# The half chunk of the second layer's hidden blocks moves from its end to its start, and the residual's rows are formed on TensorE

## The reference, cut to what matters

```python
# _L1_cond_ref: x is x1, per sequence b an expert e = lora_indices[b], rank 16, SCALE 0.5
gate = x @ W_gate.T + SCALE * (x @ A_gate[e].T) @ B_gate[e].T      # 512 -> 1376
up   = x @ W_up.T   + SCALE * (x @ A_up[e].T)   @ B_up[e].T
act  = silu(gate) * up
down = act @ W_down.T + SCALE * (act @ A_down[e].T) @ B_down[e].T  # 1376 -> 512
# _L1_ffn_ref on down:
xn = down * rsqrt(mean(down * down) + EPS)
xq = round-and-clip of xn to 8 bits by its row's largest value
wq = ternary W
y  = xq @ wq.T + b
return x1 + (down + gelu(y))
```

## Time and profile before

| | before |
|---|---|
| median of 3 runs | 1140.66 us (1136.92 to 1141.06) |
| the profiled execution | 1140.98 us |
| its span, first to last instruction | 1139.1 us |
| mean granted PE clock | 0.981 |
| PE busy | 1065.4 us (94%) |
| DVE / ACT / POOL busy | 556.1 / 307.1 / 134.4 us |

### The profile page before, as it was taken

One profiled execution on the slowest core, in us unless ns is written; L12 is line 12 of the kernel. 1 busy time (PEld: TensorE's weight loads), 2 busy tenths in 40 slices (PEclk: granted clock), 3 DMA queues, 4 the chain that ended last, 5 costly groups with the idle time before them and its releaser, 6 DMA issues.

```text
span 1139.1 us, 13740 instructions
## 1 busy us (share of the span) xinstructions
PE 1065.4 (94%) x5448; PEld 896.1 (79%) x5448; DVE 556.1 (49%) x680; ACT 307.1 (27%) x489; POOL 134.4 (12%) x178
## 2 busy tenths in 40 slices
PE   1899999999999999999889999999999999988775
PEld 0788888888888888888778888888888888877652
DVE  8855454444343444434753343343343344357876
ACT  1522121212112121212432131131131131134665
POOL 4400000000000000000140010010010010024325
PEclk9899999999999999999999999999999999998887
DMA  3776010100101010010411031030030130032103
GB/s 104 238 249 234 2 56 1 55 0 0 55 0 55 0 55 0 21 71 1 148 61 42 28 100 38 28 108 31 28 110 28 28 110 28 28 110 76 45 1 148
DMA packets 25425, 71.81 MB, mean 63 GB/s; under 512 B 5235, under 2 KB 5427, under 8 KB 25267
## 3 DMA queue, kind: packets, MB, share of 16 engines
q1 hardware_dynamic: 19762, 46.24, 11.5%
q0 software_dynamic: 5632, 25.17, 7.2%
HBM read 67.06 MB, written 4.34 MB: 63 GB/s over the span
## 4 chain that ended last, share of the span: by engine, by line
PE 86%; DVE 8%; ACT 2%; issue 2%; DMA 1%; POOL 0%; DVEq 0%; ACTq 0%; POOLq 0%
PE ps_gu L137 18%; PE ps_gu L138 18%; PE ps_gu L139 18%; PE ps_d L137 8%; PE ps_d L138 8%; PE ps_d L139 8%; PE ps_t L139 1%; PE ps_t L138 1%; PE ps_t L137 1%; PE ps_gu L837 1%; DVE h_lo L1626 1%; PE ps_t L728 1%; DVE ar_lo L1443 1%; ACT a_hi L1001 1%; ACT z_new L1091 1%
## 5 line engine op out<-in xcount | busy, mean ns | idle before, releaser
L137 PE MATMUL ps_gu<-a_hi,gu_hi 128*128 128x512 f32 x800 | 316.3, 395 | 2.2 <-DVE a_lo L1312 2.2
L138 PE MATMUL ps_gu<-a_lo,gu_hi 128*128 128x512 f32 x800 | 313.7, 392 | 0.0
L139 PE MATMUL ps_gu<-a_hi,gu_lo 128*128 128x512 f32 x800 | 312.7, 391 | 0.0
L139 PEld LDWEIGHTS ps_gu<-a_hi,gu_lo 128*128 128x128 f32 x800 | 151.1, 189 | 32.4
L137 PEld LDWEIGHTS ps_gu<-a_hi,gu_hi 128*128 128x128 f32 x800 | 151.6, 190 | 31.6 <-DVE a_lo L1312 2.3
L138 PEld LDWEIGHTS ps_gu<-a_lo,gu_hi 128*128 128x128 f32 x800 | 151.7, 190 | 28.4
L1480 DVE TENSOR_TENSOR s_act<-s_act,ps_gu 128x512 f32<-128x512 f32 x44 | 30.2, 687 | 193.7 <-PE ps_gu L139 193.5
L1347 DVE TENSOR_TENSOR s_act<-s_act,ps_gu 128x512 f32<-128x512 f32 x56 | 38.4, 686 | 148.0 <-PE ps_gu L139 148.0
L311 POOL DMA_INDIRECT lr_raw<-in_tab_l,rows x48 | 45.8, 955 | 369.1 <-PE ps_t L728 346.3
L137 PE MATMUL ps_d<-h_hi,dn_hi 128*128 128x512 f32 x224 | 87.6, 391 | 0.0
L139 PE MATMUL ps_d<-h_hi,dn_lo 128*128 128x512 f32 x224 | 87.2, 389 | 0.0
(11 more groups left out here) (244 smaller groups left out, 1707.3 us busy)
## 6 DMA issues: line engine op xcount, KB each, us to landing
raw<-in_w SPq DMA_DIRECT2D x26, 768.0 KB, 5.5
toep_hi<-krev_hi SPq DMA_DIRECT2D x12, 512.0 KB, 5.7
toep_lo<-krev_lo SPq DMA_DIRECT2D x12, 512.0 KB, 6.9
acc<-in_x_t SPq DMA_DIRECT2D x4, 1024.0 KB, 11.1
out<-x1b SPq DMA_DIRECT2D x16, 256.0 KB, 2.0
toep_lo<-krev_hi SPq DMA_DIRECT2D x4, 512.0 KB, 6.1
w_all<-in_wq SPq DMA_DIRECT2D x1, 1024.0 KB, 8.2
raw<-in_wq SPq DMA_DIRECT2D x4, 256.0 KB, 4.0
```

What stands on the lines that cost most here:

```text
L137: pe.matmul(out_ap, st_hi, mv_hi, start=start, stop=False, skip_group_check=skip)
L138: pe.matmul(out_ap, st_hi, mv_lo, start=False, stop=False, skip_group_check=skip)
L139: return pe.matmul(out_ap, st_lo, mv_hi, start=False, stop=stop, skip_group_check=skip)
```

## The change

The 12 padded blocks of the second layer are put in the order 0, 11 (all zeros), 1, 2, ..., 10, and the first chunk runs block 0 alone; five full chunks follow, and the last of them is unrolled with the final stage in it. In the half chunk DVE copies ps_d and ps_t to z and td, so POOL's memsets of x1b and td fall away. `x_rows` is 32 fp32r products per tile: a 128 x 128 piece of a_hi or a_lo as stationary, a 128 x 128 identity (ident_r, made by ACT) as moving, both halves added up in ps_d; `x_sums` on POOL is gone. yb and gb are replaced by td's own rows (`y_row`), buffers get other places, and the scratch space of the software DMA queue is set to 8192 bytes. On POOL the B_down gather of a tile comes behind the next `step`, and the sums with z begin in the last chunk (`whole`). SP loads w1[0] and w1[3] first, then w1[2].

```diff
+Y_SLOT = (0, 1, 0, 1, 2, 0, 1, 2) + (3, 0, 1, 2) * 2
...
 # POOL
-                pool.memset(x1b[:], 0.0).then_inc(v_zero, 1)
...
-                pool.memset(td[:], 0.0).then_inc(q_tev, 1)
...
+                def whole(t):
+                    for s in range(4 * t, 4 * t + 4):
+                        if s in ON_VECTOR:
+                            continue
+                        pool.wait_ge(e_gb, s + 1)
+                        pool.wait_ge(e_zx, 2 * t + 1 + s % 4 // 2)
+                        pool.tensor_tensor(z[:, s], z[:, s], y_row(s), ALU.add).then_inc(e_op, 1)
...
-                def x_sums(first, end):
...
-                        pool.tensor_tensor(x_sum[s % 3].rearrange("p (k n) -> p k n", k=KB), a_hi[:, :, sl].bitcast(F32),
-                                           a_lo[:, :, sl].bitcast(F32), ALU.add).then_inc(e_xs, 1)
...
+                for t in range(NT):
+                    if t + 1 < NT:
+                        pool.wait_ge(r_bl, RL + t + 1)
+                        pool.wait_ge(r_lt, RL + t + 1)
+                        step(t + 1)
+                    if t:
+                        pool.wait_ge(q_bd, t)
+                        lora_down_rows(t)
                     if t >= 2:
+                        whole(t - 2)
+                for t in range(2, NT):
+                    whole(t)
 # PE
+                def half_gate(t):
+                    pe.wait_ge(s_silu[0], M1 + t)
+                    gate_up(ps_gu[0], 0, 0, 0, t, t + 1).then_inc(s_g[0], 1)
+
+                def half_up(t):
+                    pe.wait_ge(s_mul[0], M1 + t)
+                    gate_up(ps_gu[1], 1, 0, 0, t, t + 1).then_inc(s_u[0], 1)
+                    pe.wait_ge(q_tev, t + 1)
+                    transposes(ps_t, 1, t)
...
+                half_gate(0)
+                half_up(0)
+                for t in range(NT):
+                    if t + 1 < NT:
+                        half_gate(t + 1)
+                    down_part(0, NC0, t, M1 + t).then_inc(s_d[1], 1)
+                    pe.wait_ge(r_adl, t + 1)
+                    lora_hidden((0,), M1 + t)
+                    if t + 1 < NT:
+                        half_up(t + 1)
+                pe.wait_ge(s_silu[0], M1 + NT)
+                with pe.Fori(NC0 + 1, CL) as c:
...
-                            last = pe.transpose(ps_d[:, s, sl], x_sum[(4 * t + s) % 3][:, sl], ident_f[:])
+                        for a in (a_hi, a_lo):
+                            for k in range(KB):
+                                last = pe.matmul(ps_d[:, s % 4, k * P:(k + 1) * P], a[:, k, rows_s], ident_r[:],
+                                                 start=(a is a_hi and k == 0), stop=(a is a_lo), skip_group_check=True)
...
+                gate_0(0)
+                up_0(0)
...
                 for t in range(NT):
...
+                    gate_up(ps_gu[2], 0, 1, 1, t, RL + t + 1).then_inc(s_g[1], 1)
+                    pe.wait_ge(q_tev, RL + t + 1)
+                    transposes(ps_t, 2, RL + t)
+                    pe.wait_ge(s_silu[0], m + 1)
+                    gate_up(ps_gu[0], 1, 1, 1, t, RL + t + 1).then_inc(s_u[1], 1)
+                    if t >= 2:
+                        quantised(t - 2)
+                    if t:
+                        lora_rows(t - 1)
+                    if t >= 2:
+                        pe.wait_ge(e_wq, KB)
+                        product(4 * t - 8)
+                    if t == 3:
+                        product(4 * t - 7)
                     if t + 1 < NT:
+                        gate_0(t + 1)
+                    if t:
+                        x_rows(t - 1, 0)
...
+                    if t + 1 < NT:
+                        up_0(t + 1)
+                    if t:
+                        x_rows(t - 1, 1)
...
+                    down_part(0, CL, t, m)
...
+                    down_part(1, CL, t, m).then_inc(s_d[1], 1)
                     pe.wait_ge(r_adl, RL + t + 1)
+                    lora_hidden((0, 1), m)
+                lora_rows(3)
                 quantised(2)
+                x_rows(3, 0)
+                product(8)
+                product(9)
+                x_rows(3, 1)
+                product(10)
+                product(11)
                 quantised(3)
+                for s in range(12, NSUB):
+                    product(s)
 # ACT, half chunk
+                for t in range(NT):
+                    m = M1 + t
+                    hidden_high(0, m, t)
+                    down_rows(1, t)
+                    act.wait_ge(s_u[0], m + 1)
+                    b_split(1 if t + 1 < NT else 2, t + 1)
+                    if t + 1 < NT:
+                        gate(0, m + 1)
+                    else:
+                        next_gate_up(0, NC0)
...
 # DVE, half chunk
+                for t in range(NT):
+                    m = M1 + t
+                    up(0, m)
+                    hidden_low(0, m)
+                    down_rows(1, t)
+                    b_split(1 if t + 1 < NT else 2, t + 1)
+                    if t + 1 == NT:
+                        next_gate_up(0, NC0)
+                    dve.wait_ge(s_d[1], m + 1)
+                    dve.tensor_copy(z[:, 4 * t:4 * t + 4], ps_d[:]).then_inc(s_ev, 1)
+                    dve.wait_ge(q_td, t + 2)
+                    dve.tensor_copy(td[:, t * TT:(t + 1) * TT], ps_t[:]).then_inc(q_tev, 1)
...
 # DVE, last chunk
+                    td_masked(3)
...
+                td_low(3)
+                clip(2)
+                fresh(3)
+                largest(3)
+                whole(7)
...
+    half_first = [0, 2 * NC1 - 1] + list(range(1, 2 * NC1 - 1))
...
-    nc = bacc.Bacc("TRN2", target_bir_lowering=False, num_devices=1)
+    nc = bacc.Bacc("TRN2", target_bir_lowering=False, num_devices=1, dynamic_dma_scratch_size=8192)
```

More of the change, by code:

```diff
@@ L797, in quantised, with product @@
                         last.then_inc(e_tp, 1)
-                def ahead(t):
+                def product(s):
+                    t = s // 4
+                    pe.wait_ge(e_qt, s // 2 + 1)
+                    if s == 4:
+                        pe.wait_ge(s_mul[1], tiles(1, ML + NT))
+                    if s:
+                        pe.wait_ge(e_yb, s if s <= 4 else s - 1)
+                    if s == 5:
+                        pe.wait_ge(e_wq, KB)
+                    for k in range(KB):
+                        at = (s % 2) * L + k * P
+                        last = pe.matmul(y_bank(s), q_t(t)[:, s % 4 // 2, at:at + P], w_q[:, k],
+                                         start=(k == 0), stop=(k == KB - 1))
+                    last.then_inc(e_y, 1)
@@ L861, in _ @@
-                    pe.wait_ge(r_tdl, t + 1)
-                    pe.wait_ge(r_bdl, t + 1)
-                    for s in range(4):
-                        sl = slice(s * P, (s + 1) * P)
-                        last = mm3(pe, ps_d[:, s], h_hi[:, 1, sl], h_lo[:, 1, sl], bd_hi[:, s // 2], bd_lo[:, s // 2],
-                                   start=False, stop=True, skip=True)
-                    last.then_inc(q_bd, 1)
-                products(2, 3)
-                quantised(2)
-                x_rows(3)
@@ L1147, in gelu @@
-                def gelu(first, end):
-                    for s in range(first, end):
-                        act.wait_ge(e_yb, s + 1)
-                        if s >= GD:
-                            wait_whole(act, s - GD)
-                        act.activation(gb[:, s % GD], yb[:, s % YD], ACT.Gelu).then_inc(e_gb, 1)
-                gelu(0, 1)
+                        td_high(t - 1)
+                    hidden_high(0, m, r)
+                    gate(1, m)
+                    down_rows(2, r)
@@ new lines, in _ @@
+                    hidden_high(1, m, r)
+                    if t >= 2:
+                        keep_quantised(t - 2)
+                    if t + 1 < NT:
+                        act.wait_ge(s_u[1], tiles(1, m) + 1)
+                        b_split(2, r + 1)
+                    if t:
+                        squares(t - 1)
+                    if t + 1 < NT:
+                        gate(0, m + 1)
+                    if t:
+                        roots(t - 1)
+                    bd_split(t)
@@ L1155, in _ @@
+                td_high(3)
+                gelu(7)
+                to_bf16(2)
+                keep_quantised(2)
+                squares(3)
+                roots(3)
+                gelu(8)
+                gelu(9)
                 scaled(3)
-                gelu(1, YD)
+                gelu(10)
                 to_bf16(3)
-                gelu(YD, 5)
+                gelu(11)
                 keep_quantised(3)
-                gelu(5, NSUB)
+                for s in range(12, NSUB):
+                    gelu(s)
```

602 lines of the change are left out of this document (307 added, 295 removed).

## The result

| | before | after |
|---|---|---|
| median | 1140.14 us (4 runs) | 1153.48 us (4 runs, 1151.35 to 1154.17) |
| ratio to before, 95% interval | | 1.0119 [1.0094, 1.0143] |
| profiled execution, its span | 1140.98, 1139.1 us | 1151.35, 1149.6 us |
| PE / DVE / POOL busy | 1065.4 / 556.1 / 134.4 us | 1067.3 / 547.4 / 105.6 us |

The changed kernel is 1.2% slower; 1152 us was forecast. In a second series of six runs it took 1151.49 us, 1.0107 [1.0078, 1.0136]. The page's busy table answers to the earlier trace rows: PE has hardly more work, and POOL has lost 29 us. Neither says anything of the 13 us.

What follows compares the result with a forecast made beforehand. PE work bounds the full chunks, waits the final stage. Start 585.78 + half chunk 71.6 + four chunks 338.9 + last chunk 115.5 + stalls 10.7 + end 28.0 = 1150.5 us span, 11.4 above before: 1152 us, range 1141 to 1164.

Steps and rivals of the forecast that it cites:

- waits for b_lo, three tiles: Half chunk: PE stands 5.25 us in each of three tiles, the 8.2 us gather loop having 2.95 of cover; 15.75 us.
- after the last half tile: End of the half chunk: 2.15 us ahead of down_part, then 4.5 us before the first full chunk's gate products.
- clock in the half chunk: Half chunk: four stalls each followed by 3.2 us at half clock, losing 1.6 each; 6.4 us, bounds 0 to twice that.
- half chunk: The half chunk at its new place, first: 42.36 us of work, 22.8 of stalls, 6.4 for the clock; 71.6 us.
- stalls of the last chunk: Last full chunk with the final stage beside it: PE's remaining waits and one slow stretch, together 10.7 us.
- last chunk up to the last low-rank rows: Last full chunk with part of the final stage: 115.5 us of PE work and 10.7 of stalls.
- from there to the end: From the last low-rank rows to the kernel's end: 28.0 us against 36.7 before, eight products remaining instead of 14.
- The gathers: Rival, half chunk: the gathers are hidden, so 15.75, 4.5 and the clock's 6.4 us go; 1125 us, chance 0.12.
- the clock does fall: Rival it answers: the clock doesn't fall as idle and work alternate quickly, minus 6.4 and 1.6; 1144 us, chance 0.17.
- The lock: Rival, last chunk: POOL's adds shut out DVE's two-input subtractions, so the lock moves; 9 us, 1161 us, chance 0.13.
- That ends ... this part of the change wins about 19: Last chunk: GpSimd's sums lock DVE and stall PE; their end takes some 30 us of stalls down, winning about 19.
- The doubled products of x: Last chunk: 32 identity products per tile instead of 16 transposes, 0.11 us each, 3.5 us per tile against 1.8; 5 us.

Runs made afterwards that it cites:

- e1_early_tables: Changed kernel with the half chunk's table transposes moved right behind the gate products, so the next gather starts earlier: 1132.33 us, 0.9947 of before.
- e6_sums_in_gap: Changed kernel with GpSimd's sums and fp32 transposes instead of identity products, the sums behind b_lo of the next tile: 1152.38 us, 1.0149 of before.
- r3_gap: Second series of the changed kernel with GpSimd's sums behind the next tile's b_lo instead of identity products: 1151.62 us, 1.0106 of before.
- e8_early_and_sums: Changed kernel with both early table transposes in the half chunk and GpSimd's sums behind the next tile's b_lo instead of identity products: 1127.44 us, 0.9899 of before.
- e3_identity_alone: Kernel before with x's rows as 32 identity products and no GpSimd sums, the half chunk still at the end: 1145.6 us, 1.0045 of before.
- e7_sums_beside_low_halves: Changed kernel with GpSimd's sums instead of identity products, started right behind the next table gather, beside DVE's h_lo and b_lo: 1159.67 us, 1.0215 of before.
- r2_one_half: Second series of the changed kernel with 16 identity products per tile instead of 32, from a_hi alone: 1152.08 us, 1.0104 of before.
- e2: Changed kernel with unread products filling PE's waits in the half chunk and ahead of the first full chunk: 1149.21 us, 1.0090 of before.
- e5: Changed kernel with 16 identity products per tile instead of 32, from a_hi alone, first series: 1151.38 us.

## Why the prediction was right

| step | forecast, us | measured, us |
|---|---|---|
| waits for b_lo, three tiles | 15.75 | 5.26 + 4.96 + 5.11 = 15.33 |
| after the last half tile | 2.15 and 4.5 | 1.95 and 4.47 |
| first tile | 0.4 | 0.15 |
| clock in the half chunk | 6.4 | 6.6 (fillers against idle) |
| half chunk | 71.6 | 70.7 |
| four chunks | 338.9 | 340.6 |
| stalls of the last chunk | 1.0, 1.4, 1.4, 0.9, 1.2, 3.2, and 1.6 for the clock | 0.78, 1.33, 1.31, 0.73, 1.01, 2.89, no slow stretch |
| last chunk up to the last low-rank rows | 126.2 | 125.3 (995.4 to 1120.7) |
| from there to the end | 28.0 | 28.9 |
| start of the half chunk | 585.78 | 584.12 |

**The half chunk** went as worked out, wait by wait: the loop of the gather stood uncovered, and PE waited for its last step. The loop's four steps stood in the trace of before and could be set against the products that the new order leaves over them. **The clock** term held to 0.2 us: what it costs could be read from rows of before at the lower level. The last of the four stretches lies in the first looped chunk (0.50 from 656 to 658), which is why the four chunks take 1.7 us more than forecast; without such a stretch they take 338.92 (e1_early_tables).

**The last chunk** came out to 0.9 us because two errors cancel, which is luck: PE waits 8.25 us there, with no stretch at the lower clock, where 10.7 were forecast, and its products take 117.1 us, where 115.5 were. **The start** differs by 1.7, within what the profiles show (584.1 to 587.0 in twelve of thirteen). **The end** is 28.9 in all four profiles of kernels with this last chunk, so the 0.9 that the forecast lacks is no scatter.

**The rivals.** The gathers are not hidden (waits of 5 us), and the clock does fall. The lock does not cost anything beside the adds in the changed kernel: no subtraction takes longer beside them than elsewhere; only factors of 128x4 stand 1.0 to 1.2 us instead of 0.2 beside three adds at 1108, with t_lo waiting for other things. But the margin was thinner than the forecast's 3 us: four scalings end at 1083.41, and the next add starts at 1083.53. In e6_sums_in_gap one scaling meets an add and takes 1.52 us instead of 0.42.

**What was wrong is a reason, not a number.** "That ends ... this part of the change wins about 19" gave the gain of the last chunk to the end of GpSimd's sums. Its size was right: 18.38 us of waits and some 19 us of work at half clock, which lose half of it, became 8.25 and none: 19.7 us in all. But with the sums back the new order keeps most of it (waits of 9.6 in r3_gap, with two falls of the clock, and 10.4 in e8_early_and_sums, with none), and in the old order their end took 5.8 us off the waits and did not make the kernel faster, since doubled products and the clock took more (e3_identity_alone). The sums cost 7 to 8 us in the new order where they meet DVE's work (e7_sums_beside_low_halves). The sum came out right since its stalls were followed through the new order, with no subtraction stretched, which holds there with and without the sums. The step failed in reading the stretched h_lo ahead of PE's wait as the whole cause: taken away, PE waited for the next thing in line.

**And one term holds as work, not as time.** The doubled products of x were counted with 5 us. They cost that as work: 0.11 to 0.12 us each (1041.40 to 1041.87 for four), and PE's busy time falls by 5.2 us without them (e8_early_and_sums against e1_early_tables). What taking them away gives is less: 2.6 us up to the last low-rank rows in that pair, and nothing where PE's longer waits for td and t_lo are followed by the lower clock (r2_one_half, r3_gap). The Trainium skill's 81 ns for such a pair (TensorE: Matmul & The Clock Gate, Back-to-back issue gap) is not borne out by these rows.

## What to carry to other kernels

When work with a fixed latency loop (gather, landing, split) is moved, count the products that the new order leaves over the loop, not the work; where they are too few, start the loop earlier in the tile rather than moving the work back: that was worth 24 us of the trace here, some 20 of the median. A stretched instruction ahead of a wait is a suspect; the wait is worth something only if the next releaser in line is early, and taking out the suspect in the old order tests that, if nothing is added in its place (here doubled products were, which blurs what the run says). Work taken off an engine that already waits in the same stage may come back as a longer wait at a lower clock.

## What the runs showed of the hardware that was not expected

- Products whose result nobody reads keep the granted clock at 1.00 through waits of 5 us, and 6.6 us of following work are saved by them.
- The same wait of 2.9 us for t_lo is followed by full clock in five profiles (the changed kernel twice, e1, e2 and e8) and by half clock in four (e5, e6, r2 and r3), though e8 has the same last chunk as e6 and r3.
- Four one-input scalings in SBUF are stretched from 1.42 to 5.76 us beside GpSimd's adds of two SBUF tiles, as the two-input subtraction is.
